# Taking the softmax sums' reciprocals apart on GpSimd, the middle parts of Q and K on ScalarE, and a later place for the spread product

## The reference

```python
x = x + xcond(layernorm(x), ctx, ctx, tau, delta, ...)    # cross attention, 16 heads of 16, 120 keys
x = x + self_attention_and_moe(x, ...)                    # 256 keys, then one expert of 8 for each token
x = x + xcond(layernorm(x), ctx, ctx, tau, delta, ...)    # cross attention again
x = x + expert_choice_sets(x)                             # 32 experts x 4 sets, permutation by maxima

# each attention:
q, k, v = heads(z @ Wq + bq), heads(c @ Wk + bk), heads(c @ Wv + bv)
a = softmax((q @ k.T * tau + delta) / 4)
out = (a @ v).merge_heads() @ Wo + bo
```

## Time and profile before

| | us |
|---|---|
| median of 3 runs (lowest to highest) | 926.01 (925.89 to 927.42) |
| the profiled execution's own time | 924.24 |
| its span (first to last instruction) | 922.5 |
| PE busy in the span | 715.2 (78%) |
| DVE busy | 528.3 (57%) |
| ACT busy | 344.3 (37%) |
| POOL busy | 240.2 (26%) |

### The profile page before, as it was taken

How to read it: one execution, slowest core, us unless ns; L and a number is a source line. 1 busy time by engine, 2 the same in 40 slices (tenths; PEclk the granted TensorE clock), 3 DMA queues, 4 the chain that set the end, 5 groups by cost and what they waited for, 6 DMA issues and landing times.

```text
span 922.5 us, 15737 instructions
## 1 busy us (share of the span) xinstructions
PE 715.2 (78%) x5815; PEld 539.4 (58%) x5815; DVE 528.3 (57%) x1283; ACT 344.3 (37%) x627; POOL 240.2 (26%) x234
## 2 busy tenths in 40 slices
PE   2657888878988888730999999964677769896898
PEld 2444656555655654420898899953544546575775
DVE  3547577887888786341112222224658888564585
ACT  1324454445546544500323222203044444543323
POOL 1513243333343322222102211005334441212000
PEclk9769898999999998855999999997598888865999
DMA  4969355865466573337556486503845432071002
GB/s 152 122 81 195 60 100 75 118 95 80 76 136 71 84 161 116 128 115 149 176 178 199 140 237 172 166 26 59 102 80 78 85 68 48 14 292 60 36 3 90
DMA packets 59848, 101.94 MB, mean 111 GB/s; under 512 B 7715, under 2 KB 50147, under 8 KB 54613
## 3 DMA queue, kind: packets, MB, share of 16 engines
q1 hardware_dynamic: 57357, 95.75, 47.5%
q0 software_dynamic: 2416, 5.19, 2.8%
HBM read 55.30 MB, written 7.28 MB: 68 GB/s over the span
## 4 chain that ended last, share of the span: by engine, by line
PE 48%; DVE 24%; DMA 8%; issue 6%; ACT 6%; SPq 4%; POOL 4%; ACTq 0%; DVEq 0%; POOLq 0%
PE PS L792 8%; PE U L803 8%; PE MB L635 7%; PE MB L730 4%; DVE nma L1152 4%; PE U L708 4%; PE PS L690 3%; DVE R L1356 3%; SPq L1566 2%; PE MB L667 2%; DMA La<-Uba 2%; DMA QKa<-mTa 2%; PE MB L882 2%; PE PS L847 2%; PE MB L651 1%
## 5 line engine op out<-in xcount | busy, mean ns | idle before, releaser
L1152 DVE TENSOR_REDUCE nma<-MB 128x2 f32<-128x512 f32 (+1 forms) x192 | 123.1, 670 | 32.7 <-PE MB L667 32.2
L970 ACT ACTIVATE Pa<-PS 128x1024 f32<-128x1024 f32 (+1 forms) x96 | 97.9, 1024 | 59.2 <-PE PS L690 57.9
L667 PE MATMUL MB<-QKa 99*128 99x120 bf16 (+1 forms) x512 | 73.6, 258 | 30.8 <-DVE nma L1152 15.8
L792 PE MATMUL PS<-mzT,mw 128*128 128x128 f32 x736 | 87.5, 278 | 1.8 <-ACT mzT L992 1.8
L803 PE MATMUL U<-mw,mdT 128*128 x368 | 83.5, 380 | 4.8 <-ACT mdT L1002 2.4
L792 PEld LDWEIGHTS PS<-mzT,mw 128*128 128x128 f32 x736 | 85.4, 194 | 2.7 <-issue 2.3
L1312 DVE TENSOR_TENSOR yt<-U,mb 128x256 f32<-128x256 f32 x23 | 9.8, 425 | 120.9 <-PE U L803 120.9
L667 PEld LDWEIGHTS MB<-QKa 99*128 99x128 bf16 x512 | 38.9, 104 | 64.2 <-DVE nma L1152 28.8
L803 PEld LDWEIGHTS U<-mw,mdT 128*128 128x128 f32 x368 | 68.2, 190 | 13.8 <-issue 5.5
L1400 POOL TENSOR_TENSOR mv<-mv,vec 128x2 f32<-128x2 f32 (+1 forms) x40 | 31.1, 777 | 140.5 <-DVE mv L1103 93.3
L690 PE MATMUL PS<-QKa 101*128 101x256 bf16 (+1 forms) x384 | 61.6, 285 | 3.1 <-DMA QKa<-mTa 3.1
(11 more groups left out here) (198 smaller groups left out, 1356.8 us busy)
## 6 DMA issues: line engine op xcount, KB each, us to landing
mw<-in_mw SPq DMA_DIRECT2D x31, 1024.0 KB, 6.0
QKa<-spa SPq DMA_DIRECT2D x144, 128.0 KB, 5.0
Qb<-spb SPq DMA_DIRECT2D x48, 128.0 KB, 4.4
Oa<-Uba SPq DMA_DIRECT2D x16, 256.0 KB, 3.6
v<-in_v SPq DMA_DIRECT2D x1, 4096.0 KB, 13.8
v<-in_v SPq DMA_DIRECT2D x4, 1024.0 KB, 11.9
W<-in_W SPq DMA_DIRECT2D x3, 1280.0 KB, 6.7
yb<-yt SPq DMA_DIRECT2D x23, 128.0 KB, 1.7
```

The source lines that it names most:

```text
L667: i = e.matmul(b[:, keys * j:keys * j + keys], Q[0:99, h0 + j, 128 * qt:128 * qt + 128], K[0:99, h0 + j, 0:keys], start=True, stop=True)
L792: i = e.matmul(ps[:, 128 * f:128 * f + 128], w[:, k, 128 * f:128 * f + 128], zz[:, k, :], start=k == 0, stop=k == 1)
L970: e.activation(p[0:keys, :], ps[0:keys, :], ACT.Exp, scale=0.25).then_inc(sems["exp"], 1)
L1152: e.tensor_reduce(A.nm[qt][:, h0:h0 + heads], b[:, 0:heads * keys].rearrange("p (h s) -> p h s", h=heads), AX.X, ALU.max, negate=True).the ...
```

## The change

Four edits:

1. `sums_split` goes from VectorE to GpSimd, and takes five instructions instead of four: the second part is written twice, once to partitions 0 to 31 of a new tile `Lm` (for the subtraction) and once to its place in the stack. GpSimd also waits for the last of the five before it goes on. A new semaphore `parts` counts them; `sums_out` waits for it.
2. `split_mid` goes from VectorE to ScalarE: 40 casts in all, at the same places of the list.
3. p1 gets later times in all three layers; p2 keeps its own, but for 1.66 to 1.72 in layer 1.
4. ps gets earlier times in all layers, and p0 in layer 2.

```diff
-T_PROJECT = ((1.44, 1.57, 1.82, 2.56), (1.28, 1.36, 1.49, 1.66), (1.4, 1.5, 1.65, 2.03))
+T_PROJECT = ((1.44, 1.5, 2.1, 2.56), (1.28, 1.33, 1.6, 1.72), (1.35, 1.4, 1.8, 2.03))
...
-            self.Lp = s.ring(f"Lp{tag}_", 2, [96, 128], BF)
+            self.Lp, self.Lm = s.ring(f"Lp{tag}_", 2, [96, 128], BF), s.new(f"Lm{tag}", [32, 128], BF)
...
         def sums_out(n):
             A, b = att(n), bank("p1", n)
             g.wait_ge(f"d_sel_{tag(n)}", 16)
-            g.wait_ge("recip", 5 * count("p0", n))
+            g.wait_ge("parts", 5 * count("ps", n))
...
+        def split_mid(what, n):
+            g.wait_ge("split_r", SPLIT[what, n] + 1)
+            e.activation(parts(what, n)[1], whole(what, n)[1], ACT.Identity).then_inc(sems["split_m"], 1)
...
-        def split_mid(what, n):
-            A, k = att(n), SPLIT[what, n]
-            cols = CK2 if what == "kp" and cross(n) else 256
-            g.wait_ge("split_r", k + 1)
-            e.tensor_copy(parts(what, n)[1], whole(what, n)[1]).then_inc(sems["split_m"], 1)
...
+        def sums_split(n):
+            l, parts, mid, k = att(n).Lr[n % 2], att(n).Lp[n % 2], att(n).Lm[:, :], 5 * (count("ps", n) - 1)
+            g.wait_ge("recip", count("p0", n))
+            g.wait_ge("p1", count("p1", n) - 2)
+            e.tensor_copy(parts[0:32, :], l[:, :]).then_inc(sems["parts"], 1)
+            g.wait_ge("parts", k + 1)
+            e.tensor_tensor(l[:, :], l[:, :], parts[0:32, :], ALU.subtract).then_inc(sems["parts"], 1)
+            g.wait_ge("parts", k + 2)
+            e.tensor_copy(mid, l[:, :]).then_inc(sems["parts"], 1)
+            g.wait_ge("parts", k + 3)
+            e.tensor_copy(parts[32:64, :], l[:, :]).then_inc(sems["parts"], 1)
+            g.wait_ge("parts", k + 4)
+            e.tensor_tensor(parts[64:96, :], l[:, :], mid, ALU.subtract).then_inc(sems["parts"], 1)
+            g.wait_ge("parts", k + 5)
```

More of the change, by code:

```diff
@@ L516, in build @@
     Yn = Area(s_at).ring("Yn", 4, [128, 2, 256])
-    names = ("idb va delta tb na nb split_m v_done max_done mh recip o_scaled resid gate rank cnt rows_of own mid_b "
+    names = ("idb va delta tb na nb split_m v_done max_done mh recip parts o_scaled resid gate rank cnt rows_of own mid_b "
              "ysum back fz perm sorted_b up down turned_b added "
@@ L1047, in turn @@
                              ACT.Identity).then_inc(sems["turned_a"], 1)
-        does = {"zt": z_turn, "qp": lambda n: project_in("qp", n), "kp": lambda n: project_in("kp", n), "mt": max_turn,
+        does = {"zt": z_turn, "qp": lambda n: project_in("qp", n), "kp": lambda n: project_in("kp", n),
+                "qs": lambda n: split_mid("qp", n), "ks": lambda n: split_mid("kp", n), "mt": max_turn,
                 "sc": scores, "pv": values, "gt": gate_turn, "ro": tile_in, "be": tile_turn,
@@ L1168, in sums_inverse @@
             e.reciprocal(l[:, :], l[:, :]).then_inc(sems["recip"], 1)
[L1170 to L1180, removed]
         def sums_out(n):
@@ L1370, in vector @@
         does = {"in": copy_in, "a0": ones_and_delta, "a2": second_attention, "tb": query_bias,
-                "na": norm_stats, "nb": norm_apply, "qs": lambda n: split_mid("qp", n), "ks": lambda n: split_mid("kp", n),
-                "vp": values_in, "mx": maxima, "mh": max_split, "p0": sums_inverse, "ps": sums_split, "p1": sums_out, "p2": project_out,
+                "na": norm_stats, "nb": norm_apply,                 "vp": values_in, "mx": maxima, "mh": max_split, "p0": sums_inverse, "p1": sums_out, "p2": project_out,
                 "gl": gate_logits, "gr": gate_rank, "cnt": table, "own": own_rows, "be": tile_turn,
@@ L1480, in gpsimd @@
                 "kp": lambda n: split_rest("kp", n), "qs": lambda n: split_low("qp", n), "ks": lambda n: split_low("kp", n),
-                "of": offset, "xy": add_y, "gs": scatter, "cnt": table, "fe": fetch, "ro": tile_in, "bg": gather_back,
+                "of": offset, "ps": sums_split, "xy": add_y, "gs": scatter, "cnt": table, "fe": fetch, "ro": tile_in, "bg": gather_back,
                 "ft": front_turn, "fw": front_choice, "ex": clear}
```

## The result

The changed kernel took 914.49 us (median of four runs, 910.74 to 916.77), the kernel before beside it 925.95 us (923.51 to 927.42). The ratio is 0.9875, with a 95% interval of 0.9836 to 0.9914: 11.5 us faster. 906 us was forecast, with 893 to 922 as the range, and 19.7 us as the sum of the terms. So it is faster, and inside the range, with three fifths of the sum. Its gain lies between 11 and 18 us, by the timing. The profiled execution took 914.37 us, with a span of 912.6 us.

What follows compares the result with a forecast made beforehand. TensorE and VectorE, both nearly full, hand work to each other through three small banks. Terms of 19.7 us off the profiled 924.2 gave 904.5, plus 1.8 for the median 906.3, rounded to 906; range 893 to 922.

Steps and rivals of the forecast that it cites:

- Prices of single instructions: Moved work: GpSimd's five 2.0 us a block, ScalarE's cast 0.617 us, and the resulting shifts in engines' busy time.
- Layer 0: 4: Layer 0: two thirds of half of 16 us of spread-product waits return, less 8 times 0.2 for ACT: 4 us.
- Layer 1 until block 11: 7: Layer 1 until block 11: of 1.87 us of PE waits in DVE's chain, 1.0 a block for 7 blocks: 7 us.
- Blocks 12 to 15: 2.7: End of layer 1: first three blocks gain 1.2 us each; block 15 loses 0.9 to POOL's slower parts: 2.7 us.
- Experts' stage: 0: Experts' stage: ACT, held by two early casts, ends `mdT` about when DVE's half ended before; no gain or loss.
- Layer 2: 6: Layer 2: blocks 16 to 19 gain 1, 2, 1.7, 1.7 us, others 0.3, less 1.5 for DVE meeting POOL: 6 us.
- ACT is not short of time there, and I take 0.2 us: Layer 0: the cast delays an exponential 0.85 us, but the next starts two us later, so PE feels 0.2 us.
- GpSimd's queue.: Work behind the moved parts: bias, layer 1's low part, next powers; in layer 2 parts come at 719.8, hardly sooner than 720.3.
- For DVE operations that now meet POOL: 1.5 us: Layer 2: a deduction of 1.5 us within that layer's 6 us, for VectorE operations that now meet GpSimd's.
- The third rival: Shared port and late parts: POOL's five take 3.5 us and hold DVE's `za`, `y` or `Mh`; slower, 928 to 942; chance 0.07.
- the first one: Waits move instead of going: PE stands at the exponential or later spread product; 914 to 922 us; chance 0.24.
- The fourth: ACT's queue: each of 40 casts holds a needed exponential for 0.85 us; slower or equal, 939 us; chance 0.04.

Runs made afterwards that it cites:

- E1: The kernel before with only the later place of the spread product (eight table times), parts and casts still on VectorE: 915.12 us, ratio 0.9856.
- E3: The kernel before with only the middle casts moved to ScalarE: 933.46 us, ratio 1.0054.
- E2: The changed kernel with the old places and the casts back on VectorE, so only the parts are on GpSimd: 921.76 us, ratio 0.9932.
- E8: E4 with layer 2's parts (1.40 to 1.62) behind the subtraction of `Yz` in GpSimd's order: 911.12 us, ratio 0.9813.
- E11: E4 again, on one chip with the changed kernel: all middle casts on VectorE, 909.10 us, ratio 0.9816.
- E4: The changed kernel with the middle casts back on VectorE; parts on GpSimd and new places stay: 908.91 us, ratio 0.9811.
- E10: The changed kernel, casts on ScalarE, with layer 2's front choice step later (2.85 to 3.0): 909.64 us, ratio 0.9824.
- E12: The changed kernel a third time, no edit, as neighbour on one chip of E11 and E10: 912.01 us, ratio 0.9857.
- E9: E4 with layer 2's front choice step later (2.85 to 3.0): 905.93 us, ratio 0.9764.
- E7: E4 with the parts of layer 2 on VectorE, GpSimd having them in layers 0 and 1 alone: 907.96 us, ratio 0.9805.
- E6: The changed kernel with middle casts on ScalarE in layers 0 and 1 alone, layer 2's on VectorE: 908.53 us, ratio 0.9783.

## Why the prediction came out as it did

**Prices of single instructions: right.** Five of GpSimd 2.05 us (2.0), ScalarE's cast 0.623 (0.617), VectorE's busy time down by 43 (45), ScalarE's up by 21.5 (25), GpSimd's by 40 (35 to 50), waits for the parts at L721 8.2 us (under 15). The end of layer 1 came 14.8, 17.3 and 19.2 us earlier (14).

**"Layer 0: 4" and "Layer 1 until block 11: 7": near together, by luck.** They gave 6.1, 10.1 and 11.1 in three executions: layer 0 3.7, 7.7 and 8.9, blocks 8 to 11 2.4, 2.4 and 2.2. The second term was mis-sized by three: it counts 1.0 us for each of 7 blocks, and 8 to 11 are four. The working of the first was weak too. I gave half of 16 us of waits to layer 0 without asking the trace by stretch. There the kernel before has 6.6 us in layer 0 (3.31 at block 0, 1.64 at blocks 1 and 2) and 14.9 in layer 1, 12.8 of them at its last four blocks.

**"Blocks 12 to 15: 2.7": too small, 7.2 to 8.7 measured.** Both of its steps failed. The first three blocks gave more than 1.2 us each: their waits at L721 (1.84, 2.06 and 3.46 us) went but for 0.23; and block 15, for which 0.9 us more was forecast, waited 3.95 in place of 5.40 us. E1, with VectorE's parts, gains 7.4 us over the same blocks: it is the place.

**"Experts' stage: 0": 1.4 to 2.7 us lost, not by the change's doing there.** The stage from the first L792 to L619 took 190.2 us before and 192.9 after with the same 1164 products; E1 took 190.5, E3 193.4, E2 193.1, and E8, which has the change's parts on GpSimd, 190.5. TensorE was busy 172.6 us in it or 175.4: the last group of 16 (L803) takes 3.72 us at full clock (E8) and 5.40 where the clock has fallen.

**"Layer 2: 6": the step that failed most.** It lost 2.1 to 2.4 us instead. The later place alone gave 7.1 (E1), so the 6 us were there; with the parts on GpSimd 4.0 to 4.7 were left (E11, E4). Of block 16's wait, for which 1 us was forecast, 0.2 went. Two things were left out of the term. Both are seen in the traces, and together they don't account for the whole. *The casts.* "ACT is not short of time there, and I take 0.2 us" was read from layer 0, for the exponential. The instruction that is held is another, the copy of the turned `z`, at the start of a layer, where one projection waits for it with nothing beside it; and the low clock makes it dearer: 2 us by block 16. *GpSimd's queue.* The prediction named the bias, the low part and the powers as what stands behind the five. It missed the subtraction of `Yz`, for which VectorE's next step waits, with the maxima behind that. The section on the change has two 128 x 512 operations behind the five "that nobody waits for soon"; for the first of them that was wrong. Here it is around the spread product of block 18, in the changed kernel:

```profile
730.26 0.48 POOL L1408 CAST Lpb<-Lb 32x128 bf16<-32x128 f32 x1
...
732.02 0.42 POOL L1416 TENSOR_TENSOR Lpb<-Lb,Lmb 32x128 bf16<-32x128 f32 x1
...
732.51 1.16 POOL L1467 TENSOR_TENSOR Yz<-Yz,z 128x512 f32<-128x512 f32 x1
...
733.63 1.27 POOL L1423 TENSOR_TENSOR x<-x,W 128x512 f32<-128x512 f32 x1
...
733.71 1.48 DVE L1310 CAST z<-Yz 128x512 bf16<-128x512 f32 x1 [2.23 <-POOL Yz L1467]
...
735.30 1.14 DVE L1162 TENSOR_TENSOR Mhb<-nmb,Mhb 128x16 bf16<-128x16 f32 x1
...
736.37 0.64 DVE L1151 TENSOR_REDUCE nmb<-MB 128x4 f32<-128x480 f32 x1
...
737.07 0.58 PE L667 MATMUL MB<-Kb,Qb 99*128 99x120 bf16 x4 [2.15 <-DVE nmb L1151]
```

GpSimd is busy with the parts until 732.44, `Yz` comes at 733.67, VectorE has stood 2.23 us, its cast (1.48 us) and the split of the maxima behind it (L1162, 1.14 us where most take 0.17) are stretched beside GpSimd's operations, and TensorE waits 2.15 us for the maxima. What that costs is not settled. Four runs took most of VectorE's 15 us of stand away: E10 is 2.4 us faster than E12 with overlapping intervals (2.8 us in layer 2 of the trace), E9 gains 3.1 us more than E4 across chips (nothing in layer 2 of the trace), E8 gains no time and E7 1.1 us.

**"For DVE operations that now meet POOL: 1.5 us": about the size, and not told apart.** The cast of `Yz` went from 0.417 to 0.818 us, eight times, 3.2 us of VectorE; `zb` from 0.577 to 0.68, while `za` went from 0.557 to 0.541 and layer 1's `y` from 0.825 to 0.576. In the rows above the cast starts at 733.71, 0.08 us behind GpSimd's 1.27 us, and ends at 735.19, 0.29 us behind its end at 734.90: alone it takes 0.417 us, so it stood for nearly the whole of it. The rule of the Trainium skill ("SBUF — State Buffer", "Who interferes with whom") that was weighed against this change has it so: a cast of VectorE in a two-port mode is shut out for the whole of an instruction that GpSimd began first. The trace agrees here, though no row shows the mode of this cast. The third rival, which rests on the same stretching, did not come about: GpSimd's five took 2.05 and not 3.5 us, and `za` and `y` got no longer.

**The rivals.** The result lies where the first one was put, 914 to 922 us, in the first timing; the others, 18.2 and 14.1 us of gain, would be 907.8 and 911.9 us there, inside the forecast's 900 to 912. Its mechanism fits layer 2 ("the POOL queue of layer 2, ACT's cast"), as far as the traces go. TensorE's waits for the exponential, which it names first, only grew from 2.0 to 3.4 us. In layer 1 as a whole the gain came (11.1, 9.6 and 10.3 us for 9.7), at its last four blocks. The fourth (ScalarE's queue, 939 us) names the right queue, but the wrong instruction in it (the exponential), and its price is several times too high: 5.2 us in E3, 2.9 between E12 and E11.

**Where the gain comes from.** On one chip: the later place 13.1 us, the parts on GpSimd 6.5, both 19.4. On another the casts on ScalarE take 2.9 us of it again by the medians. My sum of 19.7 us was near to what the first two give, and that is luck: its terms missed in both directions, too small by up to 6 us for blocks 12 to 15 and too large by nearly 5 for blocks 8 to 11 and by 8 for layer 2.

**What stays open.** The gain was 11.5, 18.2 and 14.1 us in three timings. How far that is the chip and how far few runs isn't settled. E6 is not told apart by layer: its layer 2 has E4's instructions in E4's order and took 295.1 us against 288.5, with a lower granted clock (0.81 to 0.89 against 0.89 to 0.94 between 90 and 180 us into the layer). So what makes layer 2 of the changed kernel 6 to 7 us longer than E4's is open beyond the 2 us at its start, and what set the clock apart there no run shows. E6's casts together with E9's later step, a candidate for the best version, wasn't run; E9 is the fastest that was.

## What to carry to other kernels

When an operation is moved into another engine's queue, go through what stands behind it there and ask of each who waits for it, and who waits for that one; here VectorE's cast waited for what stood behind the five, and TensorE for the maxima behind that cast. A cast that takes 0.6 us on an idle engine isn't priced by its duration: it makes that engine wait for the cast's own input, and what is held is the next thing in its queue. And try each part of a change alone: on one chip a table of eight numbers gave two thirds of what place and parts gave, and the casts alone were a loss of 5.2 us.

## What the runs showed of the hardware

- Short operations of GpSimd on 32 x 128 took 0.29 to 0.30 us (casts) and 0.43 us (two operands) in the mean, with 0.06 to 0.08 us between them. 0.33 was estimated for each from long ones; the two kinds differ.
- The granted clock went with where the casts stood; why, no run shows. Over the same 30 us of layer 2 its mean was 0.70 to 0.71 in the five executions with casts on ScalarE there, and 0.80 to 0.83 in the nine others. A group of eight products of L635 took 3.78 us in E12 and 2.86 in E11.
- Layer 2 of E6 and of E4 has the same instructions in the same order and took 295.1 and 288.5 us, and blocks 0 to 11 of the changed kernel took 207.9 to 212.3. A stage read from one profile can be off by as much; that all three profiles of the changed kernel lost 2.1 to 2.4 us in layer 2 says more.
